# Self attention: the values of two key tiles in one visit of TensorE, the sums one step later

## The reference, cut to what matters

```
scores = einsum('bhqd,bhkd->bhqk', q, k) / sqrt(512)      # 16 heads of 32 channels
scores = where(allowed_pos, scores, -1e9); scores = where(causal, -inf, scores)
p   = softmax(scores, axis=-1)
out = einsum('bhqk,bhkd->bhqd', p, v)
```

## Time and profile before

| what | value |
|---|---|
| time, median of 3 runs | 3292.65 us (3292.33 to 3293.64) |
| time of the profiled execution | 3294.11 us |
| span of the profiled execution, first to last instruction | 3292.4 us |
| busy: TensorE / VectorE / ScalarE / GpSimd over the span | 92% / 54% / 37% / 59% |
| mean granted clock of TensorE | 0.955 |
| self attention, first score to last sums, about | 600 to 1220 us |

### The profile page before, as it was taken

How to read it: one execution, slowest core, us unless ns; L and a number is a source line. 1 busy time by engine, 2 the same in 40 slices (tenths; PEclk the granted TensorE clock), 3 DMA queues, 4 the chain that set the end, 5 groups by cost and what they waited for, 6 DMA issues and landing times. The chain is left out here.

```text
span 3292.4 us, 40242 instructions
## 1 busy us (share of the span) xinstructions
PE 3014.8 (92%) x15242; PEld 1978.1 (60%) x15242; DVE 1776.0 (54%) x2885; ACT 1216.4 (37%) x2305; POOL 1943.1 (59%) x1004
## 2 busy tenths in 40 slices
PE   7987997899999968969999999999968999999999
PEld 6876886444444426754444444444426888888887
DVE  4526554777777727758777777777623222222220
ACT  2202221455555532313666666656642211111111
POOL 3214334477888767644888888888877533433422
PEclk9988998799999978986999999999988999999999
DMA  6526454654445315535342424233023010110100
GB/s 207 183 91 204 166 173 152 135 113 104 107 108 120 87 42 206 205 132 106 68 88 56 100 52 100 56 84 72 11 77 118 26 39 13 39 39 26 39 13 13
DMA packets 198544, 310.24 MB, mean 94 GB/s; under 512 B 15544, under 2 KB 91832, under 8 KB 198352
## 3 DMA queue, kind: packets, MB, share of 16 engines
q1 hardware_dynamic: 198352, 307.68, 33.9%
HBM read 189.04 MB, written 117.44 MB: 93 GB/s over the span
## 5 line engine op out<-in xcount | busy, mean ns | idle before, releaser
L952 POOL TENSOR_TENSOR e_probs<-e_probs 128x2048 f32<-128x2048 f32 x160 | 732.5, 4580 | 174.8 <-ACT e_probs L1072 170.0
L1072 ACT ACTIVATE e_probs<-e_st 128x512 f32<-128x512 f32 x1024 | 554.4, 598 | 404.4 <-PE e_st L1120 394.4
L999 DVE TENSOR_REDUCE e_neg_max<-e_nat 128x1 f32<-128x1024 f32 x512 | 601.9, 1217 | 146.8 <-PE e_nat L1103 141.9
L1072 ACT ACTIVATE b_probs<-b_st 128x512 f32<-128x512 f32 (+3 forms) x768 | 340.4, 490 | 329.2 <-PE b_st L1120 318.8
L996 DVE CUSTOM_DVE_ANT_0 b_nat<-b_nat,mask_qk 128x128 f32<-128x128 f32 (+7 forms) x512 | 374.4, 782 | 95.1 <-PE b_nat L1103 93.2
L1419 POOL TENSOR_TENSOR m_hid_lo<-m_hid,m_hid_hi 128x512 fp32r<-128x512 f32 x128 | 168.3, 1315 | 390.2 <-DVE m_hid_hi L1456 390.2
L952 POOL TENSOR_TENSOR b_probs<-b_probs 128x1536 f32<-128x1536 f32 (+3 forms) x128 | 374.9, 2929 | 38.1 <-PE b_pv L1132 35.2
L1120 PE MATMUL e_st<-e_qs,e_ks 99*128 99x512 f32 x1024 | 387.2, 428 | 4.3 <-ACT e_probs L1072 2.9
L1103 PE MATMUL e_nat<-e_ks,e_qs 96*128 96x512 f32 x1024 | 343.0, 424 | 39.7 <-DVE e_neg_max L999 28.0
L1456 DVE CAST m_hid_hi<-m_hid 128x512 fp32r<-128x512 f32 x128 | 59.2, 462 | 569.5 <-ACT m_hid L1335 569.5
L1120 PEld LDWEIGHTS e_st<-e_qs,e_ks 99*128 99x128 f32 x1024 | 174.3, 188 | 258.0 <-ACT e_probs L1072 199.8
(11 more groups left out here) (191 smaller groups left out, 5115.3 us busy)
## 6 DMA issues: line engine op xcount, KB each, us to landing
b_qs<-sq_hi SPq DMA_DIRECT2D x30, 512.0 KB, 6.6
b_ks<-sk_hi SPq DMA_DIRECT2D x30, 512.0 KB, 14.1
e_qs<-cq_hi SPq DMA_DIRECT2D x30, 512.0 KB, 6.7
e_ks<-ck_hi SPq DMA_DIRECT2D x30, 512.0 KB, 14.4
d_x<-in_ctx SPq DMA_DIRECT2D x8, 1024.0 KB, 6.4
ck_hi<-d_part_hi SPq DMA_DIRECT2D x32, 256.0 KB, 6.4
ck_lo<-d_part_lo SPq DMA_DIRECT2D x32, 256.0 KB, 6.3
cv<-d_tok_out SPq DMA_DIRECT2D x32, 256.0 KB, 5.5
```

The lines of the kernel that those rows point to most:

```text
L952: pool.tensor_tensor(into, into, probs[:, home(n, k), :, first:TOK], ALU.add).then_inc(added, 1)
L999: dve.tensor_reduce(neg_max[:, u:u + 1], found, AX.XY, ALU.max, negate=True).then_inc(maxed, 1)
L1072: act.activation(probs[:, home(n, k), j, first:TOK], st_ps[:, bank_at("scores", blk), first:TOK], ACT.Exp).then_inc(exped, 1)
```

## The change

Two numbers and one loop. In the causal stage TensorE calls `weigh` only in even steps, for the two steps before (k - 2 and k - 1), one right after the other; sum_at becomes step 8 for half 0 and step 4 of the next group for half 1, one step later than before. What hangs on sum_at moves with it: the place of the sums in the turn of the banks, the inversion (steps 9 and 5), the normalising (steps 11 and 7) and the planner's busy list. LATE stays 1, so the copy of the values and GpSimd's adds keep their steps. The cross attention gets the same program as before.

```diff
     LATE = 1 if causal else 0
     diagonal = [causal and t * P >= h * TOK for h, t, _ in steps]
-    sum_at = {h: last_step[h] + LATE + 3 for h in range(HALVES)}
+
+    PAIR = 2 if causal else 1
+    sum_at = {h: last_step[h] + (5 if causal else 3) for h in range(HALVES)}
     VISIT_HEAD = 2
...
                             if j == VISIT_HEAD:
-                                if n * NS + k >= LATE:
-                                    weigh(*divmod(n * NS + k - LATE, NS))
+                                if k % PAIR == 0:
+                                    for back in range(PAIR if causal else 0, -1, -1)[:PAIR]:
+                                        if n * NS + k >= back:
+                                            weigh(*divmod(n * NS + k - back, NS))
                                 for h in range(HALVES):
                                     back, at = divmod(sum_at[h], NS)
                                     if at == k and n >= back:
                                         sum_up(n - back, h)
-                for k in range(NS - LATE, NS):
+                for k in range(NS - PAIR if causal else NS, NS):
                     weigh(N - 1, k)
                 sum_up(N - 1, HALVES - 1)
```

## The result

The changed kernel takes 3317.31 us (median of 7 runs, 3311.11 to 3330.25) against 3293.64 us for the kernel before (7 runs, 3288.57 to 3296.02): a ratio of 1.008, 95% interval 1.006 to 1.010, so 0.8% slower. Its profiled execution took 3312.04 us (span 3310.3), 17.9 us more than that of before. The forecast was 3312 by the median and 3313.6 by the profile.

A forecast was written before the change was run, and what follows sets the result against it. TensorE was taken as the bound, with VectorE close behind in bursts. Per group 2.0 us saved and 3.3 more stalls gave +1.3, over 15 groups +19.5, so 3312 us from a median of 3292.65; range 3284 to 3328.

The forecast's parts named there:

- The visit: TensorE, self attention: each chained set saves 0.33 us, six fewer visits save 2.0 us a group, 32 us in all.
- The maxima move: Planner's busy list shifts some units; the transpose in step 9 finds its maxima ready, so its 1.27 us wait goes.
- The bursts: TensorE between double visits outruns VectorE and ScalarE: stalls grow 3.3 us a group, 5.1 to 8.4; period 38.0 to 39.3.
- The sum: Self attention: +1.3 us a group over 15 groups with maxima, +19.5 us; last group taken as 0.
- GpSimd: GpSimd's adds, normalise and clears wait a step later; costed at nothing, 0 to 0.5 us a group if cover goes.
- (B): Rival: saving and stall growth cancel within 0.4 us a group, 3286 to 3299 us; chance 0.14.
- (C): Rival: GpSimd's clears of steps 9, 11 and 1 come late, 0.5 us more a group, 3320 us; chance 0.07.
- (A): Rival: VectorE's slack keeps stalls from growing, 3262 us, or 3287 with half the growth; chance of over 0.2% faster 0.22.
- (D): Rival: chained sets of values save less; 3342 us if nothing, 3332 if 0.6 us a group; chance 0.02.
- A sign that was wrong: Profile row of TensorE's maxima matmuls: 4 us or more idle for VectorE a group if the forecast is right.
- The other sign: TensorE's scores: they would wait for ScalarE, where before nearly none did; no size given.

The follow-up runs named there:

- light maxima: VectorE reduces only the first 128 keys of each unit, in both kernels: 3264.56 us for the changed kernel, 3271.80 us for the kernel before.
- other places: Changed kernel with its 32 units of maxima placed by hand instead of by the planner: 3261.34 us, ratio 0.990 to the kernel before.

## Why the prediction was right, point by point

- **The visit.** A chained set was to save 0.33; the second set of values adds 0.87 in the changed kernel too, against 1.20 alone. The Trainium skill (TensorEngine Tiling, Key Properties) has a drain at a change of mode; the trace agrees that there is a cost. Two drains of some 128 cycles, the size that the Trainium skill gives for one matmul (TensorE: Matmul & The Clock Gate, Step-by-step), would by estimate be 0.11 us, a third of the measured 0.33.
- **The maxima move.** The transpose no longer waits, as worked. With the old places it waits 1.71.
- **The bursts.** Step by step the schedule held. From visit end to visit end, forecast and measured (differences of starts in the first fence): steps 6 to 8, 8.1 and 8.13; 8 to 10, 4.9 and 4.91; 10 to 0, 5.5 and 5.52; 0 to 2, 5.3 and 5.25; 2 to 4, 8.65 and 8.50; 4 to 6, 6.9 and 6.90. Sum 39.3 and 39.2. The stops, counted from start to start over ten groups, went from 5.5 to 8.8 us; 5.1 and 8.4 were forecast.
- **The sum.** +19.5 was forecast; the profiled executions differ by 17.9, the medians by 23.7. What the forecast left out is the clock: it took 1.00 for granted, and said that a clock below it would be another cause. It is one, on top, in some executions. That the profile fell on an execution without such falls, and that the median of seven lay only 5 us above the forecast (later it was 3325 in five runs and 3313 in three), is luck.
- **GpSimd.** Costed at nothing: no clear is waited for in the changed kernel. It is close behind: with light maxima both kernels wait 1.0 us a group for its clears.
- **Rivals.** (B) and (C) did not come: the loss is clear of 0.2%, and GpSimd's clears are in time. (A), slack in VectorE serves the bursts: it does not, with the planner's places; with other places it does, and the time it priced (3262) is what that kernel shows, by coincidence: the price was the saving of the pair, and single visits reach the same without it. (D) falls with the 0.87.
- **A sign that was wrong.** I wanted 4 us or more of idle before the matmuls of maxima; the row has 2.6. I had mixed lost time, from start to start (4.4 in the table above), with the row's idle, which is smaller at each wait (1.01 for 1.27 at the transpose of before), as the modelled end of a matmul lies behind the next start. The other sign, scores that wait for ScalarE, came: 0.3 to 1.7 us.

## What to carry to other kernels

Saving fixed cost on the bounding engine by bunching its work is worth only what its neighbours can buffer: here 2.0 us a group were saved and 3.2 lost in waits, for maxima that VectorE had not reduced yet and scores that ScalarE had not taken yet. By the schedule that is because three score banks and two to four units ahead do not bridge a visit of 2 us and feed a whole step behind it; kernels with more banks or a longer reach were not run. When an engine is over 90% busy and waits in short stops, work the order of one period through by hand, with durations from rows, and hand over the long items early enough that the other engine works on them during the long job; that gave 30 us, with or without the bunching. Count lost time from start to start, not by the idle column.

## What the runs showed that was not expected

TensorE's granted clock fell to 0.5 after short stops in an otherwise full stretch. In the groups with maxima the profiles show:

| stop before the fall | kernel | followed by a fall |
|---|---|---|
| 2.00 and 1.48 us, for the rows | only the sums later | both, 13.7 us at 0.5 |
| 1.71 us, transpose | whole change, maxima where they were | 15 of 15, 3.4 us at 0.5 |
| 1.00 us, transpose | pair, sums as before | 4 of 15 |
| 1.01 us, transpose | before | 0 of 15 |
| 0.92 us, before t2 | changed, three profiles | 1 of 42 |

In the second row a visit takes 2.90 instead of 1.64 us. What sets the stops of about 1 us that are followed by a fall apart from those that are not is open: the kernel before has the same stop as the third row and none. So a wait of about 1 to 2 us can cost more than its length, and at the short end in some groups and executions only: a reason to remove such waits even where the median hardly shows them.
